# Perceiver block in float32: eight heads' row maxima taken off by the tensor engine, one quarter of the second layer's K expanded on GpSimd, ScalarE's expansions spread, rounded GELU values kept with their offset

## The chip, the cores and the metric

One core of a Trainium2 chip runs the whole block in one program. The engines are PE (TensorE, the matrix array; PEld are its weight loads), ACT (ScalarE), DVE (VectorE), POOL (GpSimd) and SP, which issues most transfers. The metric is the device time of one execution in microseconds, the median of several runs. A difference of some 0.2% is about what a measurement of this kernel can tell from none.

## The reference

The input is 64 batches of 64 tokens of width 128, with a context of 128 tokens each, 16 heads of width 8:

```python
x = x + xattn(layernorm(x), ctx, ctx, mask, Wq, Wk, Wv, Wo)      # causal: queries see keys 0..q
x = x + attn(layernorm(x), Wq, Wk, Wv, Wo, W_down, W_up_k, W_up_v)
x = x + ffn(layernorm(x), w1, b1, w2, b2)
# attn
latent = (x @ Wk + x @ Wv) @ W_down;  k = latent @ W_up_k;  v = latent @ W_up_v
scores = clip(einsum('bhqd,bhkd->bhqk', q, k) * scale, -1e4, 1e4)
scores = clip(scores * exp(-1e-4 * |q - k|), -1e4, 1e4);  out = softmax(scores) @ v @ Wo
# ffn: each linear layer rounds its input and its weights to 127 steps of their absolute maximum
out = (round(x / sx) @ round(w / sw).T + b) * (sw * sx)
h = gelu(linear(x, w1, b1));  o = linear(h, w2, b2)
```

## The kernel before, in words

Two batches make a tile of 128 rows (tokens), so there are 32 tiles per layer. Every engine's program is written out by hand and the engines meet only at semaphores. The two attention layers form one pipeline of 64 steps, called turns here: turn n computes the scores of tile n (0 to 31 are layer one, 32 to 63 layer two). Four tiles make a group j (0 to 15), for which x and the context are transposed and q, k and v projected at once. Which of these pieces is due in a turn follows from LEAD, so it depends on n mod 4: the transpose of x in turns 0 mod 4, v in 1 mod 4 (in layer one the context's transpose too), k in 2 mod 4, q in 3 mod 4.

What one turn does on PE, in this order: scores of tile n (L529); in layer two the second half of tile n-3's shift (L560); values and the sums of exponentials of tile n-3 (L575, L581); the output projection of the tile before (L591); the transposes of tile n-2 so that keys lie on partitions, heads 0 to 7 (L548) and heads 8 to 15 (L546 or L548); and the pieces due. PE's small results go through three PSUM banks used in rotation. A bank is only free once ACT has taken what it held, so the transposes of heads 0 to 7 of this turn wait for ACT's exponential (L770) of heads 8 to 15 of the tile before.

ACT does in a turn of layer two: exponential of heads 8 to 15 of tile n-3, logarithm and inverse of the sums of exponentials (L775, L781), exponential of heads 0 to 7 of tile n-2, the inverse standard deviations of a group of tiles (`root`, L676 and L678) where ROOT_TURN says so, normalising a tile for the next layer (L683 or L695), the copies of the pieces (for v four copies, L736; k L725, q L717, x L711), and last the expansions of K: `expand(j, h)` multiplies kT by a mask that keeps one head in four (L763, 128x512), four for a group, h = 0 to 3. EXPAND gives the turn, 4j minus 5, 4, 3, 2. For the groups 3 to 7, POOL makes h = 0 and 1 (L319).

DVE takes the scores out of PSUM (L958 with mask in layer one; L963, the clip, in layer two), reduces the row maxima for each head (L977; in layer two L972 for heads 0 to 11 and L974, float16, for heads 12 to 15), divides by the sums (L904), adds the residual (L898) and makes the layer norm's moments (L874, L878). POOL multiplies by the decay in layer two (L372, 128x1024) and subtracts the maxima (L380: 16 heads in layer one, HS = 12 heads, 128x768, in layer two). The maxima of the other ON_PE = 4 heads are subtracted on PE: `shift_keys` adds, into the PSUM bank with the transposed heads 8 to 15, products of the float16 maxima with minus the identity, two 128x128 matmuls for each head, four column strips side by side. For the last two tiles DVE does POOL's work (L912, L919).

To normalise tiles 16 and up for layer two, ACT needs minus mean times inverse deviation, which POOL makes (L305, L308) in the turn after `root`.

After turn 63 comes the feed-forward layer: maximum over x, rounding, 32 matmuls of 512 columns (L633), 16 GELUs of 1024 columns on ACT (L846), each followed by a maximum on DVE (L1035). Meanwhile PE puts the bias into PSUM banks 0 to 5, three one-row matmuls of 512 columns each (L638). Then the maximum of all is reduced (DVE L1038, a transpose on PE L646, L1040, a broadcast on PE L648, L1042, L1045). Rounding one of the eight groups is two steps: multiply by 1/scale and add 1536 in float16 (ACT L853 for H_ACT, DVE L1052 for the other two), which rounds to whole numbers, and subtract 1536 again into bfloat16 `hq` (DVE L1059, all eight groups). PE multiplies (L657, 16 matmuls for a group), DVE scales and adds x (L1066), SP stores.

Of the kernel before, what the change touches and what calls it, by code (L numbers as in the profile page):

```python
# [47 lines left out]
ON_PE = 4  # L48
# [5 lines left out]
H_ACT = (1, 2, 4, 5, 6, 7)  # L54
# [65 lines left out]
def perceiver_block(nc, x_in, ctx_in, mask_in, xWq, xWk, xWv, xWo, sWq, sWk, sWv, sWo, sWd, sWuk, sWuv,  # L120
                    w1_in, b1_in, w2_in, b2_in, consts, out):
    with ExitStack() as stack:
        def sb(name, shape, dt=F32):
# [39 lines left out]
        ones_b = sb("ones_b", [1, P], BF16)  # L163
# [133 lines left out]
        def _(pool):  # L297
# [110 lines left out]
        def _(pe):  # L408
# [102 lines left out]
            def scores(n):  # L511
                layer, t = layer_of(n)
                j = n // GT
                if n % GT == 0:
# [3 lines left out]
                    if RING3 <= j < NG:  # L518
                        pe.wait_ge(s["kx_pool"], expanded("pool", j + 1))
# [116 lines left out]
            def bias(g):  # L636
                for c in range(3):
                    pe.matmul(ps[:, g, :], ones_b[:, :], b2h[:, c].unsqueeze(1).to_broadcast([1, GT, D]),  # L638
                              start=(c == 0), stop=False)
            pe.wait_ge(s["b2_split"], 5)  # L640
# [5 lines left out]
            pe.transpose(ps[0:1, 6, 0:P], scal[:, 16:17], ident).then_inc(s["hred_row"], 1)  # L646
# [450 lines left out]
```

## Time and profile before

| | |
|---|---|
| median of 3 runs | 331.9 us (331.41 to 331.94) |
| the profiled execution | 333.19 us, of which the span is 331.1 us |
| busy in the span | PE 289.7, PEld 200.8, DVE 261.3, ACT 257.7, POOL 231.8 us |
| turns 0 to 63 begin | 13.3 to 268.5 us (turn 32 at 143.0) |
| last GELU ends, maximum known, last result made | 309.0, 313.0, 328.35 us |

The span runs from the first to the last instruction; some 2.1 us lie around it. The engines' busy shares are averages over stages, and no engine is busy throughout, so the table alone does not say which engine sets the pace of a stage. In the rows below a bracket at the end of a row is the time that the engine sat idle just before it, and which instruction released it.

### The profile page before, as it was taken

To read this page: it belongs to the slowest core of one execution; us is meant where nothing else is said; L and a number is where in the kernel's file an instruction comes from. 1 tells how busy PE (TensorE), PEld (TensorE's weight loads), DVE (VectorE), ACT (ScalarE), POOL (GpSimd) and SP (SyncE) were. 2 spreads that over 40 slices of the span, in tenths; PEclk is the share of its full clock that TensorE was granted. 3 is DMA by queue.
4 is the path that set the end of the run, shared out by engine and by line. 5 is a ranking of instruction groups with operands and counts; after the bars stand their busy time and mean duration, and the time that the engine had idled before them with its cause. 6 is when DMAs were issued, how large, how long until landed. Compare 5 with 4: busy or idle time off the path is not lost.

```text
span 331.1 us, 13230 instructions
## 1 busy us (share of the span) xinstructions
PE 289.7 (87%) x5520; PEld 200.8 (61%) x5520; DVE 261.3 (79%) x567; ACT 257.7 (78%) x550; POOL 231.8 (70%) x166
## 2 busy tenths in 40 slices
PE   4796979999999999999889898989898988475784
PEld 2455648676767576776567676756666767221264
DVE  1495668989888788888679796867787999679886
ACT  3485786776769978978798989899878876699592
POOL 5177676875868787789999999999889980073000
PEclk9897999999999999999999999999999999879679
DMA  8996000000000000000000000000000000000026
GB/s 190 244 223 143 3 2 2 4 2 3 5 3 2 4 2 4 4 2 2 2 4 4 4 2 2 4 2 7 2 2 4 2 4 4 2 0 0 0 65 190
DMA packets 19100, 9.51 MB, mean 29 GB/s; under 512 B 5153, under 2 KB 18786, under 8 KB 19042
## 3 DMA queue, kind: packets, MB, share of 16 engines
q1 hardware_dynamic: 18322, 8.25, 11.2%
q8 instruction: 44, 0.72, 0.9%
q10 hardware_dynamic: 720, 0.43, 0.6%
q14 instruction: 14, 0.11, 0.1%
HBM read 6.57 MB, written 2.10 MB: 26 GB/s over the span
## 4 chain that ended last, share of the span: by engine, by line
PE 57%; ACT 20%; DVE 8%; issue 8%; POOL 5%; DMA 1%; ACTq 0%; DVEq 0%; POOLq 0%
PE ps L548 10%; PE ps L529 8%; PE ps L575 7%; PE ps L591 5%; PE ps L581 5%; ACT arena L846 4%; ACT vx L736 4%; PE ps L462 4%; PE ps L453 3%; ACT pt L770 3%; PE ps L469 3%; PE ps L546 2%; ACT arena L763 2%; POOL ud L372 2%; PE ps L435 2%
## 5 line engine op out<-in xcount | busy, mean ns | idle before, releaser
L770 ACT ACTIVATE pt<-ps 128x512 f32<-128x512 f32 x128 | 75.9, 594 | 20.0 <-PE ps L548 19.5
L380 POOL TENSOR_TENSOR u<-u,mx 128x1024 f32<-128x1024 f32 x32 | 60.9, 1904 | 39.1 <-DVE mx L977 38.9
L372 POOL TENSOR_TENSOR ud<-u,con 128x1024 f32<-128x1024 f32 x31 | 73.5, 2371 | 2.4 <-DVE u L963 2.2
L958 DVE SCALAR_TENSOR_TENSOR u<-ps,rs,arena 128x1024 f32<-128x1024 f32 x32 | 41.0, 1282 | 19.2 <-PE ps L529 19.1
L963 DVE TENSOR_SCALAR u<-ps 128x1024 f32<-128x1024 f32 x32 | 39.1, 1221 | 18.5 <-PE ps L529 16.4
L529 PE MATMUL ps<-arena,qT 32*64 32x256 f32 x1024 | 44.9, 408 | 6.4 <-ACT arena L763 4.3
L380 POOL TENSOR_TENSOR ud<-ud,mx 128x768 f32<-128x768 f32 x30 | 44.2, 1474 | 2.4
L575 PE MATMUL ps<-pt,vx 128*32 128x64 f32 x2048 | 41.4, 222 | 2.5 <-DVE oT L904 2.1
L575 PEld LDWEIGHTS ps<-pt,vx 128*32 128x32 f32 x2048 | 32.5, 111 | 16.0 <-issue 10.1
L763 ACT ACTIVATE arena<-kT,cst,con 128x512 f32<-128x512 f32 x51 | 41.5, 817 | 0.3
L581 PE MATMUL ps<-pt,con 128*32 128x128 f32 x1024 | 40.0, 275 | 0.0
L977 DVE TENSOR_REDUCE mx<-u 128x16 f32<-128x1024 f32 x32 | 38.7, 1211 | 0.1
L529 PEld LDWEIGHTS ps<-arena,qT 32*64 32x64 f32 x1024 | 15.1, 132 | 33.1 <-issue 21.9
L548 PE MATMUL ps<-con,u 128*128 128x128 f32 x256 | 33.7, 274 | 0.8 <-ACT qT L717 0.5
L775 ACT ACTIVATE lden<-ps 128x128 f32<-128x128 f32 x64 | 17.6, 276 | 19.2 <-PE ps L581 18.9
L591 PE MATMUL ps<-wo,oT 128*128 128x128 f32 x128 | 31.1, 325 | 1.3 <-ACT pt L770 0.9
L972 DVE TENSOR_REDUCE mx<-u 128x12 f32<-128x768 f32 x32 | 30.2, 943 | 0.0
L548 PEld LDWEIGHTS ps<-con,u 128*128 128x128 f32 x256 | 28.8, 141 | 2.1 <-issue 1.2
L874 DVE BATCH_NORM_STATS2 stats<-x 128x6 f32<-128x128 f32 x96 | 25.7, 280 | 3.4 <-DMA x<-in_x 3.1
L591 PEld LDWEIGHTS ps<-wo,oT 128*128 128x128 f32 x128 | 19.0, 188 | 14.3 <-issue 13.6
L736 ACT COPY vx<-ps 64x256 f32<-64x256 f32 x64 | 23.4, 366 | 4.5 <-PE ps L469 3.8
L581 PEld LDWEIGHTS ps<-pt,con 128*32 128x32 f32 x1024 | 26.0, 111 | 0.0
(148 smaller groups left out, 545.3 us busy)
## 6 DMA issues: line engine op xcount, KB each, us to landing
out<-pt SPq DMA_DIRECT2D x8, 256.0 KB, 2.3
x<-in_x SPq DMA_DIRECT2D x4, 256.0 KB, 3.7
arena<-in_ctx SPq DMA_DIRECT2D x8, 128.0 KB, 4.0
x<-in_x SPq DMA_DIRECT2D x2, 512.0 KB, 6.2
arena<-in_ctx SPq DMA_DIRECT2D x4, 256.0 KB, 6.5
arena<-in_mask_BxS_if SPq DMA_DIRECT2D x2, 256.0 KB, 4.9
arena<-in_mask_BxS_if SPq DMA_DIRECT2D x4, 64.0 KB, 4.1
arena<-in_mask_BxS_if SPq DMA_DIRECT2D x2, 128.0 KB, 3.6
```

The costliest lines, as they stand in the source:

```text
L372: pool.tensor_tensor(dh, uh, decay.unsqueeze(1).to_broadcast([P, H, HALF]), ALU.mult)\
L380: pool.tensor_tensor(uh, uh, mx[:, n % 4, 0:count].unsqueeze(2).to_broadcast([P, count, HALF]), ALU.subtract)\
L529: last = pe.matmul(ps[HALF * b:HALF * (b + 1), r].rearrange("p (h k) -> p h k", h=HR)[:, :, 0:HALF], qT[rows, j % RING3, i * P + HALF * b: ...
L548: last = pe.transpose(out_t, in_t, ident)
L575: pe.matmul(ps[32 * r:32 * (r + 1), bank, HALF * b:HALF * (b + 1)], vx[:, j % RING3, b, i, r].rearrange("p c m -> p (c m)")[:, 16 * par:16 ...
L581: last = pe.matmul(ps[32 * r:32 * (r + 1), bank, P:2 * P], ones[:, par], pt[:, n % 2, 2 * r + par, :], start=(par == 0), stop=(par == 1))
L591: pe.matmul(ps[:, bank, 0:D], oT[:, n % 2], wo[:, layer], start=True, stop=True)\
L763: act.activation(kx[:, j % RING3, h].rearrange("p n k -> p (n k)"), kT[:, j % 2], ACT.Identity, bias=cst[:, 2:3], scale=heads[:, h:h + 1]) ...
L770: act.activation(pt[:, n % 2, 4 * half:4 * half + 4].rearrange("p h n -> p (h n)"), ps[:, bank, :], ACT.Exp).then_inc(s["emptied"], 1)
L958: dve.scalar_tensor_tensor(by_head(u[:, n % UB]), sc, rs[:, 0, n:n + 1], mask[:, n].unsqueeze(1).to_broadcast([P, H, HALF]), ALU.mult, ALU ...
L963: dve.tensor_scalar(by_head(u[:, n % UB]), sc, CLAMP, -CLAMP, ALU.min, ALU.max)\
L977: dve.tensor_reduce(mx[:, n % 4], by_head(u[:, n % UB]), AX.X, ALU.max)\
```

## The change

It has five parts.

1. ON_PE goes from 4 to 8, so in layer two POOL (and DVE for the last two tiles) subtracts the maxima of 8 heads instead of 12, and `shift_keys` makes 16 matmuls instead of 8. DVE's two reductions are of 8 and 8 heads instead of 12 and 4.
2. POOL makes h = 0 of the groups 8 to 15 too. ACT makes h = 1, 2, 3 of these, and EXPAND for layer two is (4, 5, 4, 2), so none falls in a turn 1 mod 4.
3. For layer one's output the moments (lag 12 to 10) and `root` (17+4g to 15+4g) come two turns earlier, and with them POOL's L305 and L308.
4. The rounded GELU values go to PE as they are, value plus 1536 in float16, without the second rounding step on DVE. PE puts minus 1536 times w2 into each PSUM bank beforehand (`offset`, 4 matmuls of 128 rows and 512 columns for a bank, for 7 banks ahead of the maximum's transpose and the eighth behind it), and the bias comes last as one matmul of 96 rows (`b2q`, filled by three small copies on ACT in turn 24). Group 6 moves from ACT to DVE, and group 0 is rounded in two halves.
5. w2's rounding on ACT in turn 23 writes its result in order and reads with a step of four float32, where it read in order and wrote with a step.

```diff
-EXPAND = (5, 4, 3, 2)
-ON_POOL = (0, 1)
+EXPAND = ((5, 4, 3, 2), (4, 5, 4, 2))
-ROOT_TURN = ((-1, 1, 4, 7, 12, 17), tuple(17 + 4 * g for g in range(8)), (46, 54, 62, 66, 69))
+ROOT_TURN = ((-1, 1, 4, 7, 12, 17), tuple(15 + 4 * g for g in range(8)), (46, 54, 62, 66, 69))
-ON_PE = 4
+ON_PE = 8
 HS = H - ON_PE
-H_ACT = (1, 2, 4, 5, 6, 7)
+H_ACT = (1, 2, 4, 5, 7)
+DVE_TAIL = (("a", 0), ("a", 3), ("f", 0), ("f", 1), ("a", 6)) + tuple(("f", g) for g in range(2, 8))
...
+        def by_pool(j):
+            return 0 if j < RING3 else 2 if j < NG else 1
...
-                for j in range(RING3, NG):
-                    for h in ON_POOL:
-                        if n == GT * j - EXPAND[h]:
+                for j in range(RING3, 2 * NG):
+                    for h in range(by_pool(j)):
+                        if n == GT * j - EXPAND[j // NG][h]:
                             expand(j, h)
...
+            def offset(g):
+                for c in range(FC):
+                    pe.matmul(ps[:, g, :], minus_off[:, :], w2qT[:, c].unsqueeze(1).to_broadcast([P, GT, D]),
+                              start=(c == 0), stop=False)
...
-            for g in range(6):
+            pe.wait_ge(s["b2_placed"], 3)
+            for g in range(7):
                 if g % 2 == 0:
                     pe.wait_ge(s["gelu_done"], 13 + g // 2)
-                bias(g)
+                offset(g)
             pe.wait_ge(s["hred_local"], 1)
...
-                pe.wait_ge(s["hq_ready"], g + 1)
+                if g in H_ACT:
+                    pe.wait_ge(s["hr_done"], H_ACT.index(g) + 1)
+                else:
+                    pe.wait_ge(s["hr_done_dve"], (1 if g == 0 else 1 + sum(e not in H_ACT for e in range(g + 1))))
                 for i in range(GT):
+                    if g == 0 and i == 2:
+                        pe.wait_ge(s["hr_done_dve"], 2)
                     for c in range(FC):
-                        last = pe.matmul(ps[:, g, i * P:(i + 1) * P], hq[:, g % 4, c, i * P:(i + 1) * P],
-                                         w2qT[:, c], start=False, stop=(i == GT - 1 and c == FC - 1))
-                last.then_inc(s["down_done"], 1)
+                        pe.matmul(ps[:, g, i * P:(i + 1) * P], h16[g % 6][:, c, i * P:(i + 1) * P],
+                                  w2qT[:, c], start=False, stop=False)
+                pe.matmul(ps[:, g, :], ones_b[:, :], b2q[:, :].unsqueeze(1).to_broadcast([96, GT, D]),
+                          start=False, stop=True).then_inc(s["down_done"], 1)
...
-                    act.activation(w2q[:, :, :].rearrange("o c p -> o p c"),
-                                   w2r[:, :].rearrange("o (p c) -> o p c", c=FC), ACT.Identity, bias=cst[:, 4:5])\
+                    act.activation(w2q[:, :, :], w2r[:, :].rearrange("o (p c) -> o c p", c=FC), ACT.Identity, bias=cst[:, 4:5])\
...
+                if n == 24:
+                    act.wait_ge(s["b2_zero"], 1)
+                    act.wait_ge(s["b2_split"], 5)
+                    for c in range(3):
+                        act.copy(b2q[32 * c:32 * c + 1], b2h[:, c]).then_inc(s["b2_placed"], 1)
...
-                for k, lag in ((1, 12), (2, LAG_ADD[1] + NT)):
+                for k, lag in ((1, 10), (2, LAG_ADD[1] + NT)):
```

The first place is ACT's program in layer two, from the v copies of a turn 1 mod 4 to the transposes' exponentials of the next turn; before (L736 the v copies, L763 an expansion, L770 the exponentials):

```order
L676 ACTIVATE ln_v<-mv,cst 128x4
L678 ACTIVATE rs<-ln_v 128x4
L683 ACTIVATE xn3T<-x,nmr,rs 128x128
L736 COPY vx<-ps 64x16x2x8 x4
L763 ACTIVATE arena<-kT,cst,con 128x512
L770 ACTIVATE pt<-ps 128x512
L775 ACTIVATE lden<-ps 128x128
L781 ACTIVATE rden<-lden 128x128
```

The same place with the change (L748 is the v copies, L775 would be an expansion, L782 the exponentials):

```order
L695 ACTIVATE xn3T<-x,nmr,rs 128x128
L748 COPY vx<-ps 64x16x2x8 x4
L782 ACTIVATE pt<-ps 128x512
L787 ACTIVATE lden<-ps 128x128
L793 ACTIVATE rden<-lden 128x128
```

The expansion between the v copies and the exponential of heads 8 to 15 is gone from this turn, and the two short instructions of `root` stand two turns earlier.

The second place is POOL's program at the start of layer two, turns 32 to 34; before (L372 decay, L380 shift, L312 normalising a tile, L305 and L308 the factor that ACT's normalising of tile 16 needs):

```order
L372 TENSOR_TENSOR ud<-u,con 128x1024
L380 TENSOR_TENSOR ud<-ud,mx 128x768
L312 TENSOR_SCALAR xn3T<-x,mv,rs 128x128
L372 TENSOR_TENSOR ud<-u,con 128x1024
L380 TENSOR_TENSOR ud<-ud,mx 128x768
L312 TENSOR_SCALAR xn3T<-x,mv,rs 128x128
L372 TENSOR_TENSOR ud<-u,con 128x1024
L380 TENSOR_TENSOR ud<-ud,mx 128x768
L305 TENSOR_SCALAR negm<-mv 128x4
L308 TENSOR_TENSOR nmr<-negm,rs 128x4
```

With the change (L378 decay, L386 shift, L316 normalising, L309 and L312 the factor, L323 an expansion):

```order
L378 TENSOR_TENSOR ud<-u,con 128x1024
L386 TENSOR_TENSOR ud<-ud,mx 128x512
L309 TENSOR_SCALAR negm<-mv 128x4
L312 TENSOR_TENSOR nmr<-negm,rs 128x4
L316 TENSOR_SCALAR xn3T<-x,mv,rs 128x128
L323 TENSOR_TENSOR arena<-kT,con 128x512
L378 TENSOR_TENSOR ud<-u,con 128x1024
L386 TENSOR_TENSOR ud<-ud,mx 128x512
L316 TENSOR_SCALAR xn3T<-x,mv,rs 128x128
```

The factor stands behind tile 32's shift instead of tile 34's, the shifts are a third shorter, and an expansion is queued in turn 32 (and in every fourth turn after it).

The third place is PE's program between the GELUs and the first two groups of the last product; before (L633 first product, L638 bias, L646 and L648 the maximum's transpose and broadcast, L657 last product):

```order
L633 MATMUL ps<-xq,w1qT 128x512 x32
L638 MATMUL ps<-b2h,ones_b 128x512 x18
L646 MATMUL ps<-con,scal 1x128
L648 MATMUL ps<-row,ones_row 128x1
L657 MATMUL ps<-w2qT,vx 128x128 x32
L638 MATMUL ps<-b2h,ones_b 128x512 x6
```

With the change (L639 first product, L645 offset, L653 and L655 transpose and broadcast, L668 last product, L670 bias):

```order
L639 MATMUL ps<-xq,w1qT 128x512 x32
L645 MATMUL ps<-w2qT,minus_off 128x512 x28
L653 MATMUL ps<-con,scal 1x128
L655 MATMUL ps<-row,ones_row 128x1
L645 MATMUL ps<-w2qT,minus_off 128x512 x4
L668 MATMUL ps<-w2qT,ud 128x128 x16
L670 MATMUL ps<-b2q,ones_b 128x512
```

Ahead of the transpose stand 28 matmuls instead of 18, of 128 rows instead of one, and behind the broadcast four more before the last product begins.

## Rows read from the trace of the kernel before

**Rows 1.** The page's chain that ended last, shares of the span by engine:

```profile
PE 57%; ACT 20%; DVE 8%; issue 8%; POOL 5%; DMA 1%; ACTq 0%; DVEq 0%; POOLq 0%
```

**Rows 2.** Timeline: PE begins the scores of turns 31, 32; 46, 47, 48 (start, us):

```profile
139.19 0.69 PE L529 MATMUL ps<-arena,qT 32*64 32x256 f32 x16
142.98 0.69 PE L529 MATMUL ps<-arena,qT 32*64 32x256 f32 x16
...
199.34 0.69 PE L529 MATMUL ps<-arena,qT 32*64 32x256 f32 x16
...
204.41 0.69 PE L529 MATMUL ps<-arena,qT 32*64 32x256 f32 x16
...
208.30 0.69 PE L529 MATMUL ps<-arena,qT 32*64 32x256 f32 x16
```

**Rows 3.** Timeline of turn 46, ACT and PE:

```profile
200.97 0.81 ACT L763 ACTIVATE arena<-kT,cst,con 128x512 f32<-128x512 f32 x1
201.06 0.49 PE L591 MATMUL ps<-wo,oT 128*128 128x128 f32 x2
201.81 0.60 ACT L770 ACTIVATE pt<-ps 128x512 f32<-128x512 f32 x1
202.55 0.63 PE L548 MATMUL ps<-con,ud 128*128 128x128 f32 x4 [1.00 <-ACT pt L770]
```

**Rows 4.** Timeline of PE: the same wait in turns 38 and 58:

```profile
169.79 0.63 PE L548 MATMUL ps<-con,ud 128*128 128x128 f32 x4 [1.01 <-ACT pt L770]
...
253.74 0.63 PE L548 MATMUL ps<-con,ud 128*128 128x128 f32 x4 [1.00 <-ACT pt L770]
```

**Rows 5.** Timeline of turn 36:

```profile
159.32 0.49 ACT L683 ACTIVATE xn3T<-x,nmr,rs 128x128 f32<-128x128 f32 x1 [2.06 <-POOL nmr L308]
...
161.54 0.66 PE L546 MATMUL ps<-con,ud 128*128 128x128 f32 x4 [1.30 <-ACT pt L770]
```

**Rows 6.** Groups by line and shape, 160 to 260 us (busy us, mean ns, idle before):

```profile
L372 POOL TENSOR_TENSOR ud<-u,con 128x1024 f32<-128x1024 f32 x25 | 59.2, 2369 | 2.4 <-DVE u L963 2.2
L380 POOL TENSOR_TENSOR ud<-ud,mx 128x768 f32<-128x768 f32 x25 | 36.9, 1474 | 2.0
```

**Rows 7.** Groups by line and shape, 60 to 130 us:

```profile
L319 POOL TENSOR_TENSOR arena<-kT,con 128x512 f32<-128x512 f32 x8 | 8.3, 1041 | 0.0
L797 ACT ACTIVATE w2q<-w2r,cst 128x512 bf16<-128x512 f32 x1 | 2.6, 2595 | 0.0
L794 ACT ACTIVATE w1q<-w1r,cst 128x512 bf16<-128x512 f32 x1 | 0.7, 739 | 0.0
```

**Rows 8.** Timeline of turn 24: PE's wait behind ACT's L797:

```profile
115.27 0.66 PE L548 MATMUL ps<-con,u 128*128 128x128 f32 x4 [0.49 <-ACT qT L717]
```

**Rows 9.** Busy time per us: PE, PEld, DVE, ACT, POOL, granted clock share, DMA:

```profile
303.00:304.00 1.00, 0.51 (x3) 0.11 (x2) 1.00 (x2) 1.00 (x2) 0.00 (x0) 1.00 0.00 0
309.00:310.00 1.00, 1.00 (x4) 0.42 (x3) 1.00 (x2) 0.00 (x0) 0.00 (x0) 0.50 0.00 0
```

**Rows 10.** Timeline: the bias and what follows it:

```profile
305.80 2.51 PEld L638 LDWEIGHTS ps<-b2h,ones_b 1*128 1x128 bf16 x13 [1.04 <-issue]
308.60 0.15 PEld L638 LDWEIGHTS ps<-b2h,ones_b 1*128 1x128 bf16 x1 [0.28 <-issue]
309.02 0.15 PEld L638 LDWEIGHTS ps<-b2h,ones_b 1*128 1x128 bf16 x1 [0.28 <-issue]
...
311.29 0.37 PE L646 MATMUL ps<-con,scal 128*1 128x128 f32 x1
```

**Rows 11.** Timeline of the end: ACT and DVE round; PE, DVE finish:

```profile
313.10 1.29 DVE L1052 TENSOR_SCALAR ud<-arena,scal 128x2048 f16<-128x2048 f32 x1
...
315.04 4.07 ACT L853 ACTIVATE ud<-arena,cst,scal 128x2048 f16<-128x2048 f32 x2
...
326.50 1.07 PE L657 MATMUL ps<-w2qT,vx 128*128 128x128 bf16 x16 [0.19 <-DVE vx L1059]
327.60 0.75 DVE L1066 SCALAR_TENSOR_TENSOR pt<-ps,scal,x 128x512 f32<-128x512 f32 x1 [0.50 <-PE ps L657]
```

More of the change, by code:

```diff
@@ L635, in _ @@
                 last.then_inc(s["up_done"], 1)
[L636 to L638 removed]
+            def offset(g):
+                for c in range(FC):
+                    pe.matmul(ps[:, g, :], minus_off[:, :], w2qT[:, c].unsqueeze(1).to_broadcast([P, GT, D]),
                               start=(c == 0), stop=False)
[L640 to L641 removed]
+            pe.wait_ge(s["b2_placed"], 3)
+            for g in range(7):
                 if g % 2 == 0:
                     pe.wait_ge(s["gelu_done"], 13 + g // 2)
[L644 removed]
+                offset(g)
             pe.wait_ge(s["hred_local"], 1)
[L646 removed]
+            pe.transpose(ps[0:1, 7, 0:P], scal[:, 16:17], ident).then_inc(s["hred_row"], 1)
             pe.wait_ge(s["hred_max"], 1)
@@ L755, in expand @@
             def expand(j, h):
[L757 removed]
+                if h == by_pool(j):
                     act.wait_ge(s["emptied"], gets_empty(("k", j)))
@@ L830, in _ @@
                 for j in range(1, 2 * NG):
-                    for h in range(HR):
-                        if RING3 <= j < NG and h in ON_POOL:
-                            continue
-                        if n == (GT * j - EXPAND[h] if j > 2 else ((1, 2, 2, 3), (5, 5, 6, 7))[j - 1][h]):
+                    for h in range(by_pool(j), HR):
+                        if n == (GT * j - EXPAND[j // NG][h] if j > 2 else ((1, 2, 2, 3), (5, 5, 6, 7))[j - 1][h]):
                             expand(j, h)
@@ L1047, in _ @@
             dve.wait_ge(s["hscale"], 3)
-            for g in range(NG + 1):
-                if g < NG:
-                    cols = slice(g * GT * P, (g + 1) * GT * P)
-                    if g not in H_ACT:
-                        dve.tensor_scalar(h16[g % 6], hidden[:, :, cols], scal[:, 19:20], ROUND16,
-                                          ALU.mult, ALU.add).then_inc(s["hr_done_dve"], 1)
-                        dve.wait_ge(s["hr_done_dve"], sum(e not in H_ACT for e in range(g + 1)))
-                    else:
-                        dve.wait_ge(s["hr_done"], H_ACT.index(g) + 1)
-                    if g >= 4:
-                        dve.wait_ge(s["down_done"], g - 3)
-                    dve.tensor_scalar(hq[:, g % 4], h16[g % 6], -ROUND16, None, ALU.add)\
-                        .then_inc(s["hq_ready"], 1)
-                if g >= 1:
-                    m = g - 1
-                    dve.wait_ge(s["down_done"], m + 1)
-                    if m >= 4:
-                        dve.wait_ge(STORED[m % 4], 16)
-                    dve.scalar_tensor_tensor(ob[:, (m % 4) * GT:(m % 4 + 1) * GT].rearrange("p t d -> p (t d)"),
-                                             ps[:, m, :], scal[:, 20:21],
-                                             x[:, m * GT:(m + 1) * GT].rearrange("p t d -> p (t d)"),
@@ new lines, in _ @@
+            for what, g in DVE_TAIL:
+                if what == "a":
+                    if g >= 6:
+                        dve.wait_ge(s["down_done"], g - 5)
+                    parts = 2 if g == 0 else 1
+                    width = GT * P // parts
+                    for part in range(parts):
+                        cols = slice(part * width, (part + 1) * width)
+                        dve.tensor_scalar(h16[g % 6][:, :, cols],
+                                          hidden[:, :, g * GT * P + part * width:g * GT * P + (part + 1) * width],
+                                          scal[:, 19:20], ROUND16, ALU.mult, ALU.add).then_inc(s["hr_done_dve"], 1)
+                else:
+                    dve.wait_ge(s["down_done"], g + 1)
+                    if g >= 4:
+                        dve.wait_ge(STORED[g % 4], 16)
+                    dve.scalar_tensor_tensor(ob[:, (g % 4) * GT:(g % 4 + 1) * GT].rearrange("p t d -> p (t d)"),
+                                             ps[:, g, :], scal[:, 20:21],
+                                             x[:, g * GT:(g + 1) * GT].rearrange("p t d -> p (t d)"),
```

28 lines of the change are left out of this document (14 added, 14 removed).

## The prediction

> **What bounds the kernel now.** I began with the chain of work that ended last, by engine [rows 1]: PE holds 57% of the span, ACT 20%, DVE 8%, POOL 5%. The reader should see that PE leads, but that a quarter of the chain runs through ACT and POOL, so the question is where PE waits. For that I read the starts of the scores, one a turn, which give each turn's length [rows 2]. Turn 31, the last of layer one, takes 142.98 - 139.19 = 3.79 us; turn 47, of the same kind (n = 3 mod 4, one projection), takes 208.30 - 204.41 = 3.89. PE goes from one piece of work to the next in both, and the 0.10 us between them is the price of the eight small shift matmuls that only layer two has. Turn 46 has the same amount of PE work as turn 47 and takes 204.41 - 199.34 = 5.07, so 1.2 us of it is waiting.
>
> The timeline of that turn [rows 3] shows why. After the v copies ACT expands K (200.97, 0.81 us), then starts the exponential of heads 8 to 15 at 201.81, and PE, idle for 1.00 us, begins its transposes at 202.55, because their bank is the one that this exponential empties. The same idle time, released by the same line, stands in turns 38 and 58 [rows 4]; between them it is in 42, 46, 50 and 54, six turns in all, each the one behind the v copies. One more place stands out: in turn 36 ACT sits idle 2.06 us until POOL has made the factor for tile 16, its later work slides, and PE waits 1.30 us [rows 5]. So layer two is a PE pipeline with seven holes that ACT makes. The end is different: ACT and DVE round and finish, PE waits for them.
>
> **ACT's turns evened out.** The expansion behind the v copies goes to another turn or to POOL. The exponential then starts when the v copies are done, 200.97 instead of 201.81, and PE's transposes can begin at 202.55 - 0.84 = 201.71. PE itself fell idle at 202.55 - 1.00 = 201.55, and at 201.65 with the longer shift. So 0.84 us comes back in each of six turns, the longer shift's price already in it: -5.0 us. The bounds: nothing if something else takes ACT's time there, and -6.0 (six times the whole idle time).
>
> **The earlier factor.** POOL makes it two turns, some 8 us, earlier, so ACT's 2.06 us wait goes, and with it most of PE's 1.30 [rows 5]. I take -1.2; bounds 0 (if POOL is later there) and -1.3. The moments that are moved add DVE work in turns 10 and 11, ahead of the reading of the scores. What hides it is PE, whose turn of 3.79 us is longer than DVE's work in most turns; without that cover it would be a few tenths once. I put it at 0.
>
> **Eight more shift matmuls in each turn.** By [rows 2] eight cost PE 0.10 us, four strips of the array working side by side. Eight more should cost the same: 32 turns less the six counted above, 26 x 0.10 = +2.6 us. Bounds: +1.5, if the last turns hide theirs behind DVE, and +7 if the second eight cost some 0.27 each turn. DVE's two reductions cover the same 16 heads as before and I leave them at 0.
>
> **POOL.** It wins 1474 - 1041 = 0.43 us a turn, taking the 128x512 product of [rows 7] as the price of the new 128x512 shift, and pays 1.04 us a group for the expansion. Per turn it goes from 2.37 + 1.47 = 3.84 us [rows 6, 7] to 2.37 + 1.04 + 0.26 = 3.67. PE's pace from turn 38 to 58 is (253.74 - 169.79) / 20 = 4.20 us [rows 4], and with five of its holes closed and fifteen longer shifts (83.95 - 4.2 + 1.5) / 20 = 4.06. So POOL stays ahead by about 0.4 us a turn. This part gives nothing by itself; it keeps POOL from becoming the next bound. The thinnest place is turns 32 and 33, where POOL also normalises tiles: my count from its durations leaves it about 1 us ahead of PE's transposes. Without that cover a turn would grow by what POOL is late.
>
> **w2's rounding** now takes 2.60 us, against 0.74 for w1's, which has the same size and no step in its operands [rows 7]. PE waits 0.49 us behind it [rows 8]. Reading with a step of 16 bytes has no row here; it lies between the two. If it is near 0.74, PE's 0.49 goes: -0.5. If it stays at 2.60: 0. I take -0.5, being unsure. The three one-row copies in the next turn come where ACT has no expansion, so they stay covered.
> The Trainium skill (SBUF — State Buffer, Specifications) speaks against this term: two accesses to one 16-byte line are needed for full bandwidth, and each step to a new line pays. Four float32 are just such a step, so by the page reading would be slowed as writing was, and the term 0. The 2.60 against 0.74 of [rows 7] agrees that an operand with a step is slow, and does not say which side pays.
>
> **The tail, first half.** Now the bias is 18 matmuls of 512 columns. Thirteen weight loads go from 305.80 to 308.60, 0.215 us each, and then they come 0.42 apart (308.60, 309.02) [rows 10]: the granted clock has fallen from 1.00 to 0.50, from 2.4 to 1.2 GHz [rows 9]. The transpose of the maxima starts at 311.29. The change puts 28 matmuls there. At 0.215 each they end at 305.8 + 6.0 = 311.8, so the transpose and everything behind it slides by about 0.6 us. Whether the clock holds is the question. Before it fell PE had run one-row matmuls without a gap; in the GELU stage, with 128-row matmuls and PE busy only half the time, it was 1.00 [rows 9]. The new ones have 128 rows, so I expect 1.00.
> The Trainium skill (TensorE: Matmul & The Clock Gate, What's actually happening) says the gate follows how busy PE has been; by that alone the one-row stretch should have stayed fast, and the trace disagrees.
>
> **The tail, second half.** The second rounding step, eight DVE instructions, is gone, and ACT becomes the pace. Its groups take 4.07 / 2 = 2.03 us [rows 11]; five from 313.65 end at 323.8. PE finishes group 5 (ready at 321.8) with 1.07 + 0.215 for the bias, then 6 (from DVE long before) and 7: 321.8 + 3 x 1.29 = 325.7, and DVE's last instruction starts at 325.8 instead of 327.60. That is -1.8 with the slide of 0.6 in it. Bounds: -2.4 without the slide; a slower clock is a rival below.
>
> **The sum.** -5.0 - 1.2 + 2.6 - 0.5 - 1.8 = -5.9 us. Against the profiled execution, 333.19 us, that is 327.3; it ran 1.3 above the median of the runs, 331.9, so for the median 326.0.
>
> **The rivals.** *The w2 copy stays slow* (the step that is read costs as the step that was written): 326.5. For it the 2.60 row; against it nothing measured.
> *The clock falls under the offsets too*, from the 14th matmul as now: 15 x 0.205 = 3.1 us more, and 0.8 for the four behind the maximum if it is still down: 329.9, or 329 if dense work brings it back in between. For it: it falls exactly there now. Against it: the GELU stage.
> *The shift costs more than 0.10*, because the second eight reach the same strips while the first run. PE is shown busy with them for longer than their successors wait; at 0.27 a turn, 26 x 0.17 = 4.4 us more: 330.4. Against: the turn lengths.
> *More comes back*: the shift hidden in DVE-bound turns, the whole idle time of 1.0 in six turns, ACT's relief in turns 51 to 57: -2.5, 323.5.
> *Slower than before*: all 32 offset matmuls run at 1.2 GHz, as after a fall just ahead of them. 32 x 0.205 = 6.6 us on the path between the last GELU and the scale: 332.6. It decides only once nearly all 32 are slow (5.9 / 0.205 = 29). For it, the tail is where the clock moves; against it, PE's stretch before is the same as now and had 1.00.
>
> **Chances.** Forecast 0.40, w2 copy slow 0.20, clock falls 0.13, dearer shift 0.10, more comes back 0.11, slower 0.06. The range takes in the rivals up to the clock's: 323.5 to 329.9; the likeliest one's own range is 325 to 327. A measurement here tells some 0.2% (0.7 us) from no change. All but the last case are faster: 0.91 faster, 0.03 same, 0.06 slower.
>
> **What would show it.** Turns 38, 42, 46, 50, 54, 58 some 4.2 us long and without the 1.00 us wait; turn 36 without POOL as releaser of ACT; turn 47 at 3.99; the transpose of the maxima at a distance of 6.0 us from the first offset matmul, at clock 1.00; the last DVE instruction about 12.2 us behind the scale instead of 14.6; the w2 copy's duration. Wrong would be: a wait of PE for POOL's shift around turns 34 to 40, a clock of 0.50 under the offsets, or the holes of ACT reappearing in the turns that received the expansions.

## The result, and the profile after

The changed kernel takes **323.9 us** (323.6 to 324.6, 4 runs), the kernel before, run beside it on the same chip, 331.9 us (331.4 to 334.8, 4 runs). The ratio of the runs is 0.973, with a 95% interval of 0.969 to 0.978 (the two medians by themselves give 0.976, inside it). The forecast was 326.0 us with a range from 323.5 to 329.9. So the change wins some 8 us instead of 5.9: the sign and most mechanisms were as forecast, several sizes were not. The profiled execution took 324.61 us (333.19 before), its span is 322.8 us (331.1 before).

The page's chain that ended last, by engine, answers to [rows 1]. PE had 57% of it before and has 75% now:

```profile
PE 75%; ACT 14%; DVE 4%; issue 3%; DMA 1%; ACTq 1%; SPq 0%; DVEq 0%
```

POOL, with 5% before, is no longer in the line. The timeline of turn 46, from the scores of that turn to those of turn 48, answers to [rows 2, 3]:

```profile
195.72 0.69 PE L535 MATMUL ps<-arena,qT 32*64 32x256 f32 x16
195.82 1.51 ACT L748 COPY vx<-ps 64x256 f32<-64x256 f32 x4 [0.35 <-PE ps L475]
197.36 0.60 ACT L782 ACTIVATE pt<-ps 128x512 f32<-128x512 f32 x1
198.10 0.63 PE L554 MATMUL ps<-con,ud 128*128 128x128 f32 x4
...
199.95 0.69 PE L535 MATMUL ps<-arena,qT 32*64 32x256 f32 x16
...
203.94 0.69 PE L535 MATMUL ps<-arena,qT 32*64 32x256 f32 x16
```

No expansion stands between the v copies (L748) and the exponential (L782) any more, and the transposes (L554) carry no wait. The turn takes 199.95 - 195.72 = 4.23 us (5.07 before), turn 47 takes 203.94 - 199.95 = 3.99 (3.89 before). Turn 36, the place of [rows 5], in PE's timeline:

```profile
156.77 0.69 PE L535 MATMUL ps<-arena,qT 32*64 32x256 f32 x16
...
158.61 0.66 PE L554 MATMUL ps<-con,ud 128*128 128x128 f32 x4
...
160.07 0.47 PE L535 MATMUL ps<-arena,qT 32*64 32x256 f32 x8
```

It takes 3.30 us, where it took 4.70. The w2 copy in ACT's timeline answers to [rows 7]:

```profile
112.25 1.28 ACT L809 ACTIVATE w2q<-w2r,cst 128x512 bf16<-128x512 f32 x1
```

Read with the step it takes 1.28 us, neither 2.60 nor 0.74. The groups of POOL from 160 to 260 us answer to [rows 6] (busy us, mean ns, idle before):

```profile
L378 POOL TENSOR_TENSOR ud<-u,con 128x1024 f32<-128x1024 f32 x27 | 64.0, 2371 | 1.9 <-DVE u L977 1.9
L386 POOL TENSOR_TENSOR ud<-ud,mx 128x512 f32<-128x512 f32 x26 | 27.1, 1042 | 2.0
L323 POOL TENSOR_TENSOR arena<-kT,con 128x512 f32<-128x512 f32 x6 | 6.2, 1040 | 0.0
```

The price of the new shift was right (1042 ns). The three add up to 97 of the 100 us: POOL hardly rests in this stretch. The windows of the clock (its share is the third number from the end) answer to [rows 9]:

```profile
278.00:279.00 1.00, 0.00 (x0) 0.00 (x0) 0.52 (x2) 0.42 (x3) 0.00 (x0) 0.99 0.00 0
279.00:288.00 9.00, 5.60 (x16) 2.62 (x17) 4.97 (x17) 6.79 (x9) 2.06 (x2) 0.50 0.01 2
299.00:312.00 13.00, 11.09 (x76) 5.60 (x77) 10.94 (x17) 8.65 (x7) 0.00 (x0) 1.00 0.01 2
```

Under the offset matmuls, from 300.10 to 306, the clock is 1.00; but ahead of the feed-forward layer it was at 0.50 from 279 us on, where in the kernel before it had been 1.00 until 287.7. Last the timeline of the tail, which answers to [rows 10, 11]:

```profile
300.10 6.20 PE L645 MATMUL ps<-w2qT,minus_off 128*128 128x512 bf16 x28 [0.58 <-ACT arena L860]
306.14 0.27 PE L653 MATMUL ps<-con,scal 128*1 128x128 f32 x1
307.19 0.16 DVE L1056 TENSOR_SCALAR scal<-ps 128x1 f32<-128x1 f32 x1 [0.47 <-PE ps L655]
...
315.70 1.07 PE L668 MATMUL ps<-w2qT,u 128*128 128x128 bf16 x16 [0.46 <-ACT u L867]
316.82 1.06 PE L668 MATMUL ps<-w2qT,ud 128*128 128x128 bf16 x16
317.93 1.06 PE L668 MATMUL ps<-w2qT,u 128*128 128x128 bf16 x16
319.25 0.75 DVE L1077 SCALAR_TENSOR_TENSOR pt<-ps,scal,x 128x512 f32<-128x512 f32 x1 [0.36 <-PE ps L670]
```

The starts of PE's scores, turn by turn, and these rows give the whole account between the two profiled executions, read against the terms of the forecast:

| stretch | forecast, us | measured, us |
|---|---|---|
| up to turn 11 | 0 | +0.2 |
| moments (turns 11, 12) and `root` (turns 18, 22) earlier | 0 | +0.25 - 0.81 = -0.6 |
| w2 copy (turn 24) | -0.5 | -0.7 |
| turn 36 | -1.2 | -1.4 |
| six turns behind the v copies | -5.0 | -5.0 |
| longer shift in the other turns | +2.6 | +1.2 |
| from turn 63 to the first feed-forward matmul | 0 | +0.6 |
| feed-forward layer's first half | 0 | 0.0 |
| from the first bias or offset matmul to DVE's last instruction | -1.8 | -2.6 |
| sum | -5.9 | -8.3 |

### The profile page after: what moved, and what is told of

It reads as the page before. It is cut to its first block, busy times and chain, and to the rows that moved or that the text cites. A ratio compares the mean times of both kernels' runs of the same rounds, so it can differ in the third digit from the quotient of the medians.

```text
span 322.8 us, 13785 instructions
## 1 busy us (share of the span) xinstructions
PE 292.3 (91%) x5792; PEld 205.0 (64%) x5792; DVE 256.5 (79%) x561; ACT 250.1 (77%) x544; POOL 226.9 (70%) x176
## 4 chain that ended last, share of the span: by engine, by line
PE 75%; ACT 14%; DVE 4%; issue 3%; DMA 1%; ACTq 1%; SPq 0%; DVEq 0%
PE ps L554 13%; PE ps L535 11%; PE ps L581 9%; PE ps L587 8%; PE ps L597 8%; PE ps L475 5%; ACT arena L860 4%; PE ps L459 4%; PE ps L468 4%; PE ps L552 4%; PE ps L566 3%; PE ps L645 2%; PE ps L441 2%; ACT arena L775 2%; DMA arena<-in_ctx 1%
## 5 line engine op out<-in xcount | busy, mean ns | idle before, releaser
L782 ACT ACTIVATE pt<-ps 128x512 f32<-128x512 f32 x128 | 75.9, 594 | 21.7 <-PE ps L554 20.7
L386 POOL TENSOR_TENSOR u<-u,mx 128x1024 f32<-128x1024 f32 x32 | 60.8, 1902 | 37.1 <-DVE mx L991 36.9
L378 POOL TENSOR_TENSOR ud<-u,con 128x1024 f32<-128x1024 f32 x31 | 73.5, 2372 | 1.9 <-DVE u L977 1.9
L535 PE MATMUL ps<-arena,qT 32*64 32x256 f32 x1024 | 44.2, 401 | 6.4 <-ACT arena L775 4.3
L775 ACT ACTIVATE arena<-kT,cst,con 128x512 f32<-128x512 f32 x43 | 34.9, 816 | 0.1
L554 PE MATMUL ps<-con,u 128*128 128x128 f32 x256 | 34.2, 278 | 0.0
L386 POOL TENSOR_TENSOR ud<-ud,mx 128x512 f32<-128x512 f32 x30 | 31.3, 1043 | 2.4
L554 PEld LDWEIGHTS ps<-con,u 128*128 128x128 f32 x256 | 29.7, 144 | 0.6 <-issue 0.6
L748 ACT COPY vx<-ps 64x256 f32<-64x256 f32 x64 | 23.5, 367 | 6.5 <-PE ps L475 5.7
L912 DVE TENSOR_TENSOR x<-ps,x 128x128 f32<-128x128 f32 x64 | 18.5, 289 | 9.3 <-PE ps L597 9.0
```

The costliest lines, as they stand in the source:

```text
L378: pool.tensor_tensor(dh, uh, decay.unsqueeze(1).to_broadcast([P, H, HALF]), ALU.mult)\
L386: pool.tensor_tensor(uh, uh, mx[:, n % 4, 0:count].unsqueeze(2).to_broadcast([P, count, HALF]), ALU.subtract)\
L535: last = pe.matmul(ps[HALF * b:HALF * (b + 1), r].rearrange("p (h k) -> p h k", h=HR)[:, :, 0:HALF], qT[rows, j % RING3, i * P + HALF * b: ...
L554: last = pe.transpose(out_t, in_t, ident)
L775: act.activation(kx[:, j % RING3, h].rearrange("p n k -> p (n k)"), kT[:, j % 2], ACT.Identity, bias=cst[:, 2:3], scale=heads[:, h:h + 1]) ...
L782: act.activation(pt[:, n % 2, 4 * half:4 * half + 4].rearrange("p h n -> p (h n)"), ps[:, bank, :], ACT.Exp).then_inc(s["emptied"], 1)
```

## The experiments

Two views were to be told apart. The first: each part does its work at its own place, as the sum says, and the sizes of the terms were off. The second: the parts cover for each other, POOL above all. Theories A and B in an expectation are that run's own. Each ratio is against the kernel before, run on the same chip. Its median in the three rounds of measuring was 332.8 (12 runs), 333.1 (23) and 333.8 (11); the changed kernel's own ratio is 0.973.

**The longer shift taken back**, the rest of the change kept:

```diff
-ON_PE = 8
+ON_PE = 4
```

> The changed kernel with ON_PE back at 4: 8 shift matmuls a turn, POOL subtracts the maxima of 12 heads, everything else as changed. Theory A (POOL would be the next bound): POOL then needs 2.37 + 1.47 + 0.26 = 4.10 us a turn, against a mean turn of 3.93 us in the changed kernel (turns 37 to 62), so it falls behind by 0.17 or more in each and PE waits for its shift after some turns: 325.5 to 328 us. Theory B (POOL has room, the shift matmuls are pure cost to PE): about 15 turns shorter by 0.10 us, 322.5 us.

It took 335.6 us, ratio 1.008 (1.005 to 1.011): slower than the kernel before. Theory A had the right cause but ended at 328 us, 7.6 too low; theory B is out. The waits of PE (total us, times, longest) now begin with a line that the changed kernel doesn't have:

```profile
PE ps L554 <- POOL ud L386: 8.0, 15, 1.3
```

and the timeline shows POOL's shift directly ahead of PE's wait:

```profile
171.01 1.47 POOL L386 TENSOR_TENSOR ud<-ud,mx 128x768 f32<-128x768 f32 x1
172.53 0.42 PEld L554 LDWEIGHTS ps<-con,ud 128*128 128x128 f32 x4 [1.05 <-POOL ud L386]
```

Turn 63 begins at 270.0 us instead of 262.1, 7.9 us later, about the 8.0 us of these waits. Behind it 3.3 us more are lost, where POOL's last factors are made (timeline of POOL, DVE and those who wait):

```profile
274.70 0.96 DVE L926 TENSOR_TENSOR ud<-ud,mx 128x768 f32<-128x768 f32 x1 [0.78 <-POOL ud L378]
274.76 0.99 POOL L309 TENSOR_SCALAR negm<-mv 128x8 f32<-128x8 f32 x1
275.58 1.22 DVE L933 TENSOR_TENSOR ud<-u,con 128x1024 f32<-128x1024 f32 x1
275.84 1.02 POOL L312 TENSOR_TENSOR nmr<-negm,rs 128x8 f32<-128x8 f32 x1
276.89 0.88 ACT L707 ACTIVATE xn<-x,nmr,rs 128x128 f32<-128x128 f32 x2 [3.20 <-POOL nmr L312]
...
278.31 0.66 PE L552 MATMUL ps<-con,ud 128*128 128x128 f32 x4 [1.93 <-ACT pt L782]
```

In the changed kernel the same two instructions of POOL come before DVE's long ones and are short:

```profile
263.92 0.23 POOL L309 TENSOR_SCALAR negm<-mv 128x8 f32<-128x8 f32 x1
264.23 0.20 POOL L312 TENSOR_TENSOR nmr<-negm,rs 128x8 f32<-128x8 f32 x1
```

So the four heads more on PE (eight shift matmuls more) are worth some 11.7 us to the changed kernel. The second view is right: the longer shift covers for the expansions on POOL.

**POOL's expansions and the turns of the expansions taken back**, the rest kept:

```diff
-EXPAND = ((5, 4, 3, 2), (4, 5, 4, 2))
+EXPAND = ((5, 4, 3, 2), (5, 4, 3, 2))
...
-            return 0 if j < RING3 else 2 if j < NG else 1
+            return 0 if j < RING3 else 2 if j < NG else 0
```

> The changed kernel with ACT making all four expansions of the groups 8 to 15, at the turns 4j minus 5, 4, 3, 2 as before. Theory A (the expansion behind the v copies makes the hole): the six turns 38, 42, 46, 50, 54, 58 grow by 0.84 us each, 328.9 us. Theory B (the saving came from another part, the earlier root or a shorter shift on POOL): under 1 us slower.

329.3 us, ratio 0.989 (0.985 to 0.992). The six turns are back at 5.07, 5.50 and 4.21 us, and with them the wait, in turn 46 this one:

```profile
200.29 0.63 PE L554 MATMUL ps<-con,ud 128*128 128x128 f32 x4 [0.89 <-ACT pt L782]
```

Theory A had it right: these holes are ACT's, and worth 5 us.

**Moments and `root` taken back**, the rest kept:

```diff
-ROOT_TURN = (..., tuple(15 + 4 * g for g in range(8)), ...)
+ROOT_TURN = (..., tuple(17 + 4 * g for g in range(8)), ...)
...
-                for k, lag in ((1, 10), (2, LAG_ADD[1] + NT)):
+                for k, lag in ((1, 12), (2, LAG_ADD[1] + NT)):
```

> The changed kernel with root for layer one's output at turns 17+4g and moments at lag 12 again. Theory A (the ledger of turn lengths: turn 36 -1.40, turns 18 and 22 -0.38 and -0.43, turns 11 and 12 +0.25): 1.9 to 2.0 us slower, 325.8 us. Theory B (as the prediction had it, only turn 36 counts): 1.2 us slower, 325.0 us.

324.8 us, ratio 0.977 (0.973 to 0.981), an interval that overlaps that of the whole change. The trace decides: turn 36 is 4.36 us instead of 3.30, turns 18 and 22 are 4.17 and 4.25 instead of 3.79 and 3.82, turns 11 and 12 some 0.25 us shorter together. That is 1.06 + 0.81 - 0.25 = 1.6 us for this part, of which the forecast had the first alone. Theory A had the places; it took the whole 1.40 of turn 36 for this part's.

**The w2 copy taken back**, the rest kept:

```diff
-                    act.activation(w2q[:, :, :], w2r[:, :].rearrange("o (p c) -> o c p", c=FC), ...)
+                    act.activation(w2q[:, :, :].rearrange("o c p -> o p c"),
+                                   w2r[:, :].rearrange("o (p c) -> o p c", c=FC), ...)
```

> The changed kernel with w2's rounding writing with a step and reading in order, as before. Theory A (turn 24's 0.71 us is this copy's): the copy takes 2.6 us instead of 1.28 and the kernel is 0.7 to 1.2 us slower, 324.6 to 325.0 us. Theory B (turn 24 is shorter because of the earlier root): within 0.3 us of the changed kernel.

324.6 us, ratio 0.975 (0.972 to 0.979), not to be told from 0.973 by the time. In the timeline the copy is slow again and PE waits behind it:

```profile
111.63 2.61 ACT L809 ACTIVATE w2q<-w2r,cst 128x512 bf16<-128x512 f32 x1
...
114.72 0.66 PE L554 MATMUL ps<-con,u 128*128 128x128 f32 x4 [0.95 <-ACT qT L729]
```

Turn 24 takes 4.53 us (3.37 in the changed kernel, 4.08 before). The size is more than the 0.71 us between the kernels before and after, because the earlier `root` falls in turn 23, ahead of the copy, in these two kernels: the old copy starts 0.41 us behind PE's scores here, and 0.02 us ahead of them in the kernel before. Theory A has the place right.

**Only the tail left as before**: the kernel before with parts 1, 2, 3 and 5 of the change, so all of the change except the `offset` code.

> The kernel before with parts 1, 2, 3 and 5 of the change, and its old tail (second rounding step, bias ahead). Theory A (the traces: 21.8 us from the first bias matmul to the last DVE instruction became 19.2): 2.6 us slower than the changed kernel, 326.5 us. Theory B (the prediction's sum): 1.8 us slower, 325.7 us.

326.7 us, ratio 0.981 (0.977 to 0.985). Turn 63 begins at 262.1 us, as in the changed kernel; from the first bias matmul (299.52) to DVE's last instruction (321.29) it takes 21.77 us, against 19.15 in the changed kernel. The tail is worth 2.6 us, as theory A had it.

**The old bias with 128 rows.** The kernel before, with its three one-row bias matmuls replaced by 128-row ones whose other 127 rows are zero:

```diff
-        b2h = sb("b2h", [1, 3, D], BF16);  ones_b = sb("ones_b", [1, P], BF16)
+        b2h = sb("b2h", [P, 3, D], BF16);  ones_b = sb("ones_b", [P, P], BF16)
...
-                    pe.matmul(ps[:, g, :], ones_b[:, :], b2h[:, c].unsqueeze(1).to_broadcast([1, GT, D]),
+                    pe.matmul(ps[:, g, :], ones_b[:, :], b2h[:, c].unsqueeze(1).to_broadcast([P, GT, D]),
...
```

> The kernel before, its 18 + 6 bias matmuls with 128 rows instead of one (127 of them zero), same columns and same result. Theory A (the one-row matmuls let the clock fall): the granted clock stays at 1.00 through them, they end some 1.4 us earlier, the transpose starts right behind DVE's maximum, 0.5 to 1.2 us faster than before. Theory B (the clock falls here whatever PE does): 0.50 from the same place, no difference.

332.0 us, ratio 0.998 (0.996 to 1.001). The timeline shows the 18 matmuls in 4.04 us (they took 5.52 before) and the transpose behind them waiting for DVE's maximum, no longer for PE:

```profile
306.93 4.04 PE L640 MATMUL ps<-b2h,ones_b 128*128 128x512 bf16 x18 [0.58 <-ACT arena L848]
312.05 0.27 PE L648 MATMUL ps<-con,scal 128*1 128x128 f32 x1 [1.08 <-DVE scal L1040]
```

The windows over it have the clock at 1.00 throughout; before, it was 0.50 from 309 to 310 us [rows 9]:

```profile
308.00:309.00 1.00, 1.00 (x6) 0.49 (x5) 1.00 (x2) 1.00 (x2) 0.00 (x0) 1.00 0.00 0
309.00:310.00 1.00, 1.00 (x7) 0.45 (x5) 1.00 (x2) 1.00 (x1) 0.00 (x0) 1.00 0.00 0
310.00:311.00 1.00, 0.97 (x5) 0.24 (x3) 1.00 (x2) 0.07 (x1) 0.00 (x0) 1.00 0.00 0
```

From the first bias matmul to DVE's last instruction it takes 20.82 us instead of 21.77. That the rows of the operands, and not how busy PE is, made the difference here is shown: PE is as busy in either. It is one profiled execution, but the 28 offset matmuls of 128 rows kept 1.00 as well in the six traces that have them. The clock of this run falls later, though: it was 0.50 from 317 to 319 us, in the last product, after PE had been idle for 2.56 us. The gain in time, 0.2%, is at the edge of its interval.

**The longer shift alone, POOL's expansions alone, and the two together.** Parts 1 and 2 on the kernel before. First part 1:

```diff
-ON_PE = 4
+ON_PE = 8
```

> The kernel before with part 1 alone (ON_PE = 8). Theory A (PE sets the pace, POOL is not the bound of the kernel before): turns without a wait grow by 0.10 us, those behind the v copies don't, 1.2 to 2.6 us slower, 333.1 to 334.5 us. Theory B (POOL was bounding layer two): faster.

333.4 us, ratio 1.002 (0.998 to 1.006): no difference. Turn 36 is 3.38 us (POOL's shorter shift lets it make the factor in time, without the earlier `root`), twelve of the others are 0.1 longer: the gain of 1.3 us in the one place pays for the cost in the others. Then part 2:

```diff
-EXPAND = (5, 4, 3, 2)
-ON_POOL = (0, 1)
+EXPAND = ((5, 4, 3, 2), (4, 5, 4, 2))
...
+        def by_pool(j):
+            return 0 if j < RING3 else 2 if j < NG else 1
...
```

> The kernel before with part 2 alone (a quarter of layer two's K on POOL, ACT's turns evened out). Theory A (POOL at 4.10 us a turn is over what PE would need without the holes, and each expansion delays a shift): POOL's shift becomes what PE waits for; the holes' 5.0 us are lost again and more, 332 to 337 us. Theory B (the parts add up): 5.0 us faster, 326.9 us.

340.0 us, ratio 1.021 (1.016 to 1.026), slower than either theory had it. The six holes are closed (4.23 us), but turns 36, 40, 44 and 48 take 5.66, 5.34, 4.92 and 4.91. The timeline of turn 36 shows the way that POOL's lateness takes, through the factor and ACT:

```profile
160.13 0.20 POOL L311 TENSOR_TENSOR nmr<-negm,rs 128x4 f32<-128x4 f32 x1
...
160.37 0.49 ACT L686 ACTIVATE xn3T<-x,nmr,rs 128x128 f32<-128x128 f32 x1 [3.02 <-POOL nmr L311]
...
162.58 0.66 PE L549 MATMUL ps<-con,ud 128*128 128x128 f32 x4 [2.03 <-ACT pt L773]
```

Between the two profiled executions turn 63 begins 2.5 us later (271.0 against 268.5), the stretch from there to the first feed-forward matmul is 3.2 us longer (24.92 against 21.72), and the tail 1.4 us, where the clock was at 0.50 for longer.

Last parts 1 and 2 together (both diffs):

> The kernel before with parts 1 and 2 only (16 shift matmuls a turn on PE, and POOL's expansions of h = 0 in the groups 8 to 15). Theory A (the two parts give only together: part 1 frees the 0.43 us a turn of POOL that part 2 spends): the six turns behind the v copies are 4.23 us, turn 36 about 3.4, the others 0.1 longer; turn 63 starts about 5 us earlier than now (-5.0 for six turns, -1.3 for turn 36, +1.2 for the longer shift), ratio 0.984 to 0.985. Theory B (the effects add: +0.2% for part 1, +2.1% for part 2): ratio 1.02. A third case would be that POOL still binds in turns 32 to 40, because the factor for tile 16 on comes two turns later than in the changed kernel: turn 36 near 4.4 and ratio 0.988.

329.7 us, ratio 0.988 (0.984 to 0.991), turn 36 at 4.38 us, turn 63 at 264.56: the third case, with its ratio. The effects don't add: one part costs nothing, the other 2.1%, and together they win 1.2%.

**Six heads on PE instead of eight**, the rest of the change kept:

```diff
-ON_PE = 8
+ON_PE = 6
```

> The changed kernel with the maxima of 6 heads subtracted on PE instead of 8 (12 small matmuls a turn, POOL's shift 128x640). Theory A (POOL is the hidden bound): POOL takes 2.37 + 1.26 + 0.26 = 3.89 us a turn against PE's 4.0, and waits of PE for its shift appear in some turns, above all in turns 32 to 44 where POOL normalises too, and a late end as in the run with 4 heads: 325 to 330 us, between the changed kernel's 323.9 and the 335.6 of 4 heads. Theory B (POOL still has room, and PE wins 0.05 us a turn): 323 us.

327.8 us, ratio 0.982 (0.978 to 0.987), as theory A there had it. PE waits for POOL's shift 1.4 us in all, in five places, and 24.04 us pass from turn 63 to the first feed-forward matmul instead of 22.34.

**Fewer offsets ahead of the maximum.** The changed kernel with the offsets of five banks ahead of the transpose, those of 5, 6 and 7 later:

```diff
-            for g in range(7):
+            for g in range(5):
...
-                if g == 0:
+                if g == 2:
                     pe.wait_ge(s["hscale"], 1)
-                    offset(7)
+                    offset(5)
+                if g == 4:
+                    offset(6)
+                if g == 5:
+                    offset(7)
```

> The changed kernel with the offsets of five PSUM banks ahead of the transpose of the maxima instead of seven; those of banks 5, 6 and 7 are computed behind the maximum, while PE waits for rounded groups. Theory A (PE's 28 matmuls hold back the transpose, and PE has idle time behind the scale): the transpose comes up to 1.7 us earlier, but not before DVE's maximum is ready, so only until that becomes the bound, and the time falls by 0.5 to 1.5 us: ratio 0.971 or 0.969 against 0.973. Theory B (PE is already the bound behind the scale, its groups 1.11 us apart from the first rounded group to the last): what is taken from ahead comes back behind, no change, 0.973.

323.3 us, ratio 0.969 (0.965 to 0.973), against 0.973 (0.969 to 0.978): the intervals overlap. The timeline shows the transpose of the maxima, the scale and DVE's last instruction:

```profile
303.98 0.27 PE L653 MATMUL ps<-con,scal 128*1 128x128 f32 x1 [0.64 <-DVE scal L1056]
...
305.04 0.16 DVE L1060 TENSOR_SCALAR scal<-ps 128x1 f32<-128x1 f32 x1 [0.47 <-PE ps L655]
...
318.22 0.75 DVE L1081 SCALAR_TENSOR_TENSOR pt<-ps,scal,x 128x512 f32<-128x512 f32 x1 [0.36 <-PE ps L674]
```

The first offset starts at 298.86, so the transpose comes after 5.12 us instead of 6.04; but behind the scale it takes 13.18 us instead of 12.06, and the tail as a whole 19.36 against 19.15. Theory B: what is taken from ahead comes back behind. The profiled run was faster earlier (turn 63 at 261.7, and 21.57 us from there to the first feed-forward matmul), at places that this edit doesn't touch.

## Why the prediction was right in kind and short in size

The step that failed is the term of the longer shift, "32 turns less the six counted above, 26 x 0.10 = +2.6 us": the runs showed +1.2. Two more terms were mis-sized, the tail (-2.6 instead of -1.8) and moments with `root` (-0.6 instead of 0), and POOL's lead was misjudged. One by one:

*The six holes*: right. Each turn is 0.84 shorter, the longer shift's price in it, and taking part 2 back brings them back.

*Turn 36*: right in place, -1.4 instead of -1.2. With the factor in time PE has no wait for ACT left there (it had 1.30 us). On the kernel before the shorter shift does it nearly alone (3.38 us); once POOL has the expansions as well the earlier `root` is needed (4.38 and 4.36 us without it). No run has the earlier `root` alone.

*The longer shift*: the price of 0.10 us was right, the multiplier of 26 was not. Turns 32 to 34 hold no shift matmuls (the first stand in turn 35), and four of the 32 sets come behind the start of turn 63. From turn 35 on twelve turns are 0.09 to 0.11 longer and turn 40 is 0.05; the other eight outside the six and turn 36 are not. Four of these (35, 51, 53, 55) have a wait for ACT, and it shrinks by as much; turn 62 even gets 0.11 shorter, its wait of 0.26 us for DVE gone; in 37, 57 and 60 the traces show no wait, and what hides the cost there stays open. Turn 53, from PE's timeline of the kernel before:

```profile
231.36 0.46 PE L591 MATMUL ps<-wo,oT 128*128 128x128 f32 x2 [0.57 <-ACT pt L770]
```

and of the changed kernel:

```profile
226.45 0.46 PE L597 MATMUL ps<-wo,oT 128*128 128x128 f32 x2 [0.46 <-ACT pt L782]
```

So the term was +1.2, not +2.6. I had a bound of +1.5 ("if the last turns hide theirs behind DVE"); of the hidden ones DVE accounts for one turn and ACT for four.

*Moments and root*: "I put it at 0" was wrong, for I looked only at what the move adds on DVE and at its effect in turn 36. In turns 17 and 21 it also takes `root` from a place ahead of the v copies, which are late there. ACT's and PE's timeline of the kernel before in turn 17 and behind it:

```profile
88.24 0.28 ACT L676 ACTIVATE ln_v<-mv,cst 128x4 f32<-128x4 f32 x1
88.55 0.21 ACT L678 ACTIVATE rs<-ln_v 128x4 f32<-128x4 f32 x1
88.66 1.49 ACT L736 COPY vx<-ps 64x256 f32<-64x256 f32 x4
...
90.90 1.06 PE L548 MATMUL ps<-con,u 128*128 128x128 f32 x8 [0.15 <-ACT scal L740]
```

In the changed kernel the first two are gone and the v copies begin at 88.66 all the same, though the kernel is 0.4 us later there: turn 18 gets these 0.4 us back, and turn 22 the like. The moments cost 0.25 us, the root gives 0.8 (in the run with both taken back turns 11, 12, 18 and 22 have their old lengths).

*w2's copy*: the term of -0.5 became -0.7, at a duration of 1.28 us. The rule of the Trainium skill (SBUF — State Buffer, Specifications) that spoke against the term holds in part: a reading step costs, 1.28 against 0.74, but much less than the writing step, 2.60. The rival "stays slow" is out. The 0.7 is the copy's: turn 24 is 3.37 us with the new copy both with the earlier `root` and with the old one.

*The tail*: the slide of 0.6 came as forecast (6.04 against 5.46 us to the transpose), and the clock stayed at 1.00 under the offsets. Two sizes were off. The step from the transpose to the scale took 1.05 us instead of 1.36 at the full clock (-0.3, not thought of). And the last three groups on PE follow each other after 1.11 us, where I had put 1.07 + 0.215 = 1.29: the 1.07 of one group's row contains the end of its pipeline, which the next work hides. The bias matmul starts 0.90 us behind its group:

```profile
316.60 0.38 PE L670 MATMUL ps<-b2q,ones_b 96*128 96x512 bf16 x1
```

So adding the bias to 1.07 counted too much, 3 x 0.18 = 0.5 us. Together 0.8, the gap between -1.8 and -2.6.

*POOL*: the prices of its long instructions were right, and "about 1 us ahead" in the thinnest place was near (0.72 us, in turn 36). "POOL stays ahead by about 0.4 us a turn" was wrong. The sum of 3.67 us left out the factor for ACT's normalising, L309 and L312, 0.22 + 0.20 us in every fourth turn, and short gaps, and PE's pace was taken up to turn 58, with the longer turns from 51 on. From the starts of POOL's decays of tiles 37 and 45 the changed kernel's POOL takes 3.82 us a turn, and PE takes 3.95 from turn 38 to 50: POOL wins 0.13 us a turn, no more. "This part gives nothing by itself" is right, but the text never priced the loss of that cover. The lead is the time from the end of POOL's shift of a tile to PE's first transpose of its values, worked out from the rows of the timeline for turns 34 to 63:

| kernel | POOL a turn by the prices, us | POOL a turn, measured | PE a turn, 38 to 50 | least lead, us | lead in turn 47 | ratio |
|---|---|---|---|---|---|---|
| before | 3.84 | 4.00 | 4.09 | 0.79 (turn 36) | 3.55 | 1 |
| changed | 3.67 | 3.82 | 3.95 | 0.72 (turn 36) | 1.85 | 0.973 |
| changed, 6 heads on PE | 3.89 | 4.03 | 4.04 | 0.05 (turn 36 and 9 more) | 0.06 | 0.982 |
| changed, 4 heads on PE | 4.10 | 4.24 | 4.24 | 0.05 (turn 36 and 14 more) | 0.05 | 1.008 |

A lead of 0.05 us means that PE starts when POOL ends. With 6 heads on PE, 3.89 us by the prices seems to be enough against PE's 3.95; but POOL's timeline repeats every four turns at a distance of 16.13 us, 4.03 a turn,

```profile
183.36 2.37 POOL L378 TENSOR_TENSOR ud<-u,con 128x1024 f32<-128x1024 f32 x1
...
199.49 2.36 POOL L378 TENSOR_TENSOR ud<-u,con 128x1024 f32<-128x1024 f32 x1
```

so there, with no lead left in turn 36, POOL sets the pace. The 70% that the page gives POOL over the span hides this: from 160 to 260 us it is 97% by the groups above.

*What I left out*: +0.6 us between turn 63 and the feed-forward layer, where the clock fell 9 us earlier than in the kernel before. No run ties it to the change: the same stretch took 21.57 us in the run with five offsets, 21.80 with the old w2 copy and 22.48 with part 2 taken back, and 22.69 on the kernel before with part 1. What makes the clock fall sooner or later there stays open.

*The rival "more comes back"*, with 323.5, came nearest to the time. Of its three items the hidden shift came; the other two (the whole idle time of the six turns, ACT's relief in turns 51 to 57) did not come. "Slower", "the clock falls" and "the shift costs more" found nothing in the trace.

## What to carry to other kernels

An engine that makes its results ahead of the one that sets the pace has a lead, and the lead in its thinnest turn, not its busy share over the span, says what may be added to it: here 0.22 us a turn more on POOL cost 0.9% and 0.43 us cost 3.5%. Its pace is read from the distance at which its work repeats, for a sum of the long instructions leaves out the short ones. Before a part is priced at nothing because it only "makes room", price the kernel without it. A small cost on the bounding engine counts only in turns in which it doesn't wait, and a row's duration counts its pipeline's end, so the pace of like work in a queue is read from the distance of its starts.

## What the runs showed of the hardware

- One-row bias matmuls cost TensorE its clock and 128-row ones didn't. With nothing but the rows changed, the 18 matmuls ahead of the transpose took 4.04 us at a granted clock of 1.00 instead of 5.52. In each of the five profiled executions with the one-row bias the clock was at 0.50 from within these matmuls on, and their tails took 21.77, 21.77, 23.22, 23.45 and 24.30 us from the first of them to DVE's last instruction; the six with all 28 of the 128-row offsets ahead of the transpose kept 1.00 under them and took 19.15 us, all of them (the tail's other changes are in that too).
- POOL's two small instructions (128x8) took 0.99 and 1.02 us instead of 0.23 and 0.20 while DVE ran subtractions and products with two operands in SBUF. The Trainium skill (SBUF — State Buffer, Who interferes with whom) tells of such interference between these two engines, and the rows agree: POOL's two end at 275.75 and 276.86 us, within 0.1 us of DVE's beside them (275.66 and 276.80). No run here isolates it.
- ACT's conversion of 128x512 float32 to bfloat16 takes 0.74 us without a step in its operands, 1.28 us reading with a step of four float32, and 2.61 us writing with a step.
